# Attention scores as three rounded products, whole key blocks added on GpSimd, and a rewritten plan in a float32 chain of four attention layers

## The reference

```python
x = x + _L0_attn_a_ref(_layernorm(x, axis=-1), ...)   # "squared"
x = x + _L0_ffn_ref(_layernorm(x, axis=-1), ...)      # "gated"
x = x + _L0_attn_b_ref(_layernorm(x, axis=-1), ...)   # "mqa"
x = x + _L0_ffn_ref(_layernorm(x, axis=-1), ...)      # "gated"

# squared
q = _feature_map(q, gamma, beta)
k = _feature_map(k, gamma, beta)
q = q * D ** (-0.5)
attn = jnp.einsum('bqhd,bkhd->bhqk', q, k) ** 2
attn = jnp.where(mask, attn, 0.0)
o = jnp.einsum('bhqk,bkhd->bqhd', attn, v)
z = jnp.sum(attn, axis=-1)
o = o / (jnp.swapaxes(z, 1, 2)[..., None] + EPS)
return o.reshape(b, t, H * D) @ Wo.T

# gated
idx = jnp.argmax(gating, axis=-1)
k_shared = jnp.einsum('bth,bthd->btd', indicator, k)
v_shared = jnp.einsum('bth,bthd->btd', gating_top1, v)
att = jnp.einsum('bhqd,bkd->bhqk', q, k_shared) * (1.0 / math.sqrt(hd))
att = jax.nn.softmax(jnp.where(causal[None, None, :, :], att, -jnp.inf), axis=-1)
y = jnp.einsum('bhqk,bkd->bhqd', att, v_shared)

# mqa
scores = jnp.einsum('bqhd,bkd->bhqk', q, k) * scale
attn = jax.nn.softmax(jnp.where(causal[None, None], scores, min_val), axis=-1)
ctx = jnp.einsum('bhqk,bkd->bqhd', attn, v)
out = jnp.einsum('bsd,ed->bse', ctx, out_w) + out_b
```

## Time and profile before

| | us |
|---|---|
| median of 3 runs | 4801.09 |
| profiled execution | 4810.55 |
| its span | 4808.8 |
| PE busy / DVE busy / ACT busy / POOL busy | 4292.6 / 1770.6 / 1546.9 / 847.3 |
| mean granted PE clock, share of full speed | 0.961 |

### The profile page before, as it was taken

How to read it: one execution, slowest core, us unless ns; L and a number is a source line. 1 busy time by engine, 2 the same in 40 slices (tenths; PEclk the granted TensorE clock), 3 DMA queues, 4 the chain that set the end, 5 groups by cost and what they waited for, 6 DMA issues and landing times.

```text
span 4808.8 us, 76616 instructions
## 1 busy us (share of the span) xinstructions
PE 4292.6 (89%) x32674; PEld 1781.0 (37%) x32674; DVE 1770.6 (37%) x2666; ACT 1546.9 (32%) x1985; POOL 847.3 (18%) x1495
## 2 busy tenths in 40 slices
PE   6899999996999898898898989989899897988987
PEld 4343434333333333333333333333333333333333
DVE  1222212122544444434444443443443444444342
ACT  1433333340223323323333333332222233232333
POOL 1311212121101211202112221211112012011012
PEclk8999999998999999999999999999999999999999
DMA  1001010003000100101001010000001001010010
GB/s 62 18 1 36 18 36 18 18 18 102 18 1 1 54 1 23 32 1 38 16 23 32 12 43 1 25 30 26 28 1 46 9 1 54 1 37 17 1 36 27
DMA packets 63405, 115.67 MB, mean 24 GB/s; under 512 B 8672, under 2 KB 9184, under 8 KB 63072
## 3 DMA queue, kind: packets, MB, share of 16 engines
q1 hardware_dynamic: 63072, 110.77, 7.2%
HBM read 77.19 MB, written 33.55 MB: 23 GB/s over the span
## 4 chain that ended last, share of the span: by engine, by line
PE 58%; DVE 6%; issue 5%; ACT 3%; DMA 2%; POOL 2%; POOLq 0%; SPq 0%; DVEq 0%; ACTq 0%
PE banks L1085 14%; PE banks L1043 10%; PE banks L995 9%; PE banks L1027 8%; PE banks L988 7%; DVE maxima_soft L811 5%; PE banks L1024 3%; ACT probs_soft L732 3%; PE banks L1052 2%; PE banks L1184 2%; DMA tiles_soft<-out 1%; PE banks L1159 1%; PE banks L1094 1%; POOL tiles_soft L637 0%; POOL rest_soft L705 0%
## 5 line engine op out<-in xcount | busy, mean ns | idle before, releaser
L811 DVE TENSOR_REDUCE maxima_soft<-banks 128x2 f32<-128x1024 f32 (+3 forms) x1152 | 1036.6, 953 | 1309.8 <-PE banks L1052 828.6
L732 ACT ACTIVATE probs_soft<-banks 128x1024 f32<-128x1024 f32 (+1 forms) x960 | 848.5, 936 | 1252.4 <-PE banks L1027 1250.2
L1043 PE MATMUL banks<-k_soft,q_soft 32*128 32x512 f32 (+3 forms) x4608 | 547.0, 544 | 69.6 <-ACT probs_soft L732 67.6
L646 POOL TENSOR_SCALAR_AFFINE_SELECT probs_soft<-probs_soft 128x512 f32<-128x512 f32 x384 | 239.2, 635 | 1963.5 <-ACT probs_soft L732 1961.8
L1027 PE MATMUL banks<-q_soft,k_soft 32*128 32x512 f32 (+3 forms) x4608 | 487.1, 505 | 0.0
L1085 PE MATMUL banks<-probs_soft,v_soft 128*32 128x512 f32 (+3 forms) x4608 | 435.6, 497 | 13.4 <-ACT shift_soft L718 9.5
L1085 PE MATMUL banks<-probs_soft,ones 128*32 128x512 f32 (+3 forms) x4608 | 433.5, 495 | 0.0
L732 ACT ACTIVATE probs_squared<-banks 128x1024 f32<-128x1024 f32 (+1 forms) x320 | 282.8, 936 | 387.7 <-PE banks L1027 387.6
L1043 PEld LDWEIGHTS banks<-k_soft,q_soft 32*128 32x128 f32 x4608 | 187.1, 186 | 320.1 <-issue 302.3
L1024 PE MATMUL banks<-shift_soft,ones 32*128 32x512 bf16 (+3 forms) x2304 | 202.3, 339 | 113.9 <-DVE maxima_soft L811 100.9
L995 PE MATMUL banks<-g_wv,xnT_soft 128*128 128x512 f32 x512 | 251.4, 625 | 27.4 <-DVE inverse_soft L917 21.2
(11 more groups left out here) (151 smaller groups left out, 4218.7 us busy)
## 6 DMA issues: line engine op xcount, KB each, us to landing
tiles_soft<-out SPq DMA_DIRECT2D x96, 256.0 KB, 2.9
rest_soft<-out SPq DMA_DIRECT2D x96, 256.0 KB, 3.0
out<-rest_soft SPq DMA_DIRECT2D x96, 256.0 KB, 2.0
tiles_squared<-in_x SPq DMA_DIRECT2D x32, 256.0 KB, 2.9
rest_squared<-in_x SPq DMA_DIRECT2D x32, 256.0 KB, 2.9
out<-rest_squared SPq DMA_DIRECT2D x32, 256.0 KB, 2.0
raw_wq<-in_squared_wq SPq DMA_DIRECT2D x1, 1024.0 KB, 6.2
raw_wk<-in_squared_wk SPq DMA_DIRECT2D x1, 1024.0 KB, 8.5
```

The source lines that it names most:

```text
L646: ins = pool.affine_select(out=cells, in_=cells, compare_op=ALU.is_ge, fill=0.0, base=0, pattern=[[0, HG], [1, P]], channel_multiplier=-1)
L732: act.activation(slot(ph, n)[:, 2 * a:2 * a + 2, 0:width], score_pair(e, a)[:, :, 0:width], ACT.Exp if soft else ACT.Square, scale=SCALE). ...
L811: ins = dve.reduce_max(m["maxima"][:, ph % 2, 2 * a:2 * a + 2, t, p], score_pair(e, a)[:, :, col:col + P * blocks], AX_X)
L1043: ins = pe.matmul(psum[:, score_bank(e, i), col:col + P * blocks], m["q"][D * i:D * i + D, ph % NG, P * t:P * t + P], k_of(ph)[D * i:D * i ...
```

## The change

1. Queries and keys are kept as two float32r numbers, a rounded high part and the rest. ACT writes the high part from PSUM; DVE then subtracts it from the same bank and writes the low part, and only then is the bank free. Squares of them on POOL are an add and a multiply.
2. Each score product is three float32r products, high by high, high by low and low by high, in place of one float32 product. They stay in four 32-row groups.
3. No product is narrower than 256 columns: the narrow key products are widened to 256 and their surplus is not read. There are ten row bursts in place of nine, cut the same way.
4. For part B in the softmax layers POOL adds the four whole blocks of weights into `full_sum` (three adds of 128 by 2048), and "sm" for B is one block in place of four.
5. `SLOTS` 6 to 5, `TILES` 4 to 3, `Y_RING` 6 to 5, queries kept for three phases in place of four; the plan (`VALUES_AT`, `WEIGHT`, `spread`'s lists, `norm_events`) is rewritten, and "sm" B of a softmax phase is one whole unit.

```diff
-SLOTS = 6
-TILES = 4
-Y_RING = 6
+SLOTS = 5
+TILES = 3
+Y_RING = 5
 V_RING = 3
+QK_RING = 3
+PAIRS = [(HIGH, HIGH), (HIGH, LOW), (LOW, HIGH)]
...
-    (0, "A", [(1, 128, 384, 0), (3, 384, 128, 384)]),
-    (0, "A", [(2, 256, 256, 0)]),
+    (0, "A", [(1, 128, 384, 0)]),
+    (0, "A", [(2, 256, 256, 0), (3, 256, 256, 256)]),
...
-VALUES_AT = {"C": 1, "A": 8, "B": 14}
+VALUES_AT = {"C": 0, "A": 6, "B": 14}
...
-WEIGHT = {"keys": 1.3, "rows": 1.2, "av": 3.2, "sm": 3.2, "q": 3.5, ...
+WEIGHT = {"keys": 1.0, "rows": 0.9, "av": 3.2, "sm": 3.2, "q": 3.5, ...
...
+    elif soft and n > FULL[0]:
+        pool.wait_ge(sg.probs_ready, 2 * (of_kind[e] + 1))
+        if n == FULL[1] and ph:
+            wait_work(pool, ("sm", ph - 1, part))
+        elif n > FULL[1]:
+            pool.wait_ge(sg.probs_added, additions(ph, n) - 1)
+        before = slot(ph, FULL[0])[:] if n == FULL[1] else m["full_sum"][:]
+        pool.tensor_tensor(m["full_sum"][:], before, slot(ph, n)[:], ALU.add).then_inc(sg.probs_added, 1)
...
+    elif u in ("q", "q2", "k2", "ks", "kt"):
+        out, bias = split_target(e)
+        wait_work(act, e)
+        act.activation(out[:, HIGH], work[:, bank(e), :], ACT.Copy).then_inc(sg.high_ready, 1)
...
+    elif u in ("q", "q2", "k2", "ks", "kt"):
+        out, bias = split_target(e)
+        dve.wait_ge(sg.high_ready, high_parts[e])
+        ins = dve.tensor_tensor(out[:, LOW], work[:, bank(e), :], out[:, HIGH].bitcast(F32), ALU.subtract)
+        ins.then_inc(sg.work_free[bank(e)], 1)
...
-    for i in range(HG):
-        ins = pe.matmul(psum[:, score_bank(e, i), col:col + width],
-                        k_of(ph)[D * i:D * i + D, P * kb:P * kb + P],
-                        m["q"][D * i:D * i + D, ph % NG, CHUNK * c + q0:CHUNK * c + q0 + width],
-                        start=not soft, stop=True)
+    for x, (a, b) in enumerate(PAIRS):
+        for i in range(HG):
+            ins = pe.matmul(psum[:, score_bank(e, i), col:col + width],
+                            k_of(ph)[D * i:D * i + D, a, P * kb:P * kb + P],
+                            q_of(ph)[D * i:D * i + D, b, CHUNK * c + q0:CHUNK * c + q0 + width],
+                            start=(x == 0 and not soft), stop=(x == len(PAIRS) - 1))
...
+    if u == "sm" and soft and part == "B":
+        pe.wait_ge(sg.probs_added, additions(ph, FULL[-1]))
+        for i in range(HG):
+            ins = pe.matmul(out[D * i:D * i + D, :], k["ones"][:], m["full_sum"][:, i, :], start=True, stop=True)
+        products = []
```

More of the change, by code:

```diff
@@ L6 @@
 F32 = mybir.dt.float32
+F32R = mybir.dt.float32r
 BF16 = mybir.dt.bfloat16
@@ L73, with behind, blocks_seen @@
          "mxt", "rs", "rw", "out")
+def behind(c, kb, q0):
+    return max(P * (kb - TPC * c) - q0, 0)
 def parts_of(part):
     bursts = [n for n, burst in enumerate(KEY_BURSTS) if burst[1] == part]
-    products = sorted((kb, q0, width, n, col) for n in bursts for kb, q0, width, col in KEY_BURSTS[n][2])
-    return bursts, products
+    products = []
+    for n in bursts:
+        c = KEY_BURSTS[n][0]
+        for kb, q0, width, col in KEY_BURSTS[n][2]:
+            cut = behind(c, kb, q0)
+            products.append((kb, q0 + cut, width - cut, n, col + cut))
+    return bursts, sorted(products)
+def blocks_seen(t, p, blocks):
+    return min(blocks, t - TPC * p + 1)
 def norm_events(s):
-    events = [("stats", s, t) for t in range(3)]
+    events = [("load", s, t) for t in range(TILES)] + [("stats", s, t) for t in range(TILES - 1)]
     for t in range(NT):
-        if t + 3 < NT:
-            events.append(("stats", s, t + 3))
+        if t + TILES - 1 < NT:
+            events.append(("stats", s, t + TILES - 1))
         events.append(("ln", s, t))
@@ L588, in _ @@
         def _(sp):
-            stores = [Count() for _ in range(TILES)]
             for e in events:
```

241 lines of the change are left out of this document (141 added, 100 removed).

## The result

The changed kernel takes 4859.05 us (median of 4 runs, 4856.71 to 4860.78), the kernel before, run beside it, 4801.55 (4797.94 to 4805.5). The ratio is 1.0119, with a 95% interval of 1.0102 to 1.0137. Forecast were 4680 us and a range from 4550 to 4880: the time lies in the range, the direction was wrong, and faster had been given 0.72.

What follows compares the result with a forecast made beforehand. PE's own work was taken to set the time (busy 4292.6 us). Work -291, bank waits +62, split +25, adds +10, tiles +45, first act +25 make -124 us from 4810.55, so 4687, stated as 4680; range 4550 to 4880.

Steps and rivals of the forecast that it cites:

- +49 wider products: PE's key and row products: widening 128 columns to 256 adds work, netted inside the savings of -96 and -84 us.
- +45 tiles: Tile loads and outputs: three tiles need three rounds for eight, eleven stage changes at 4 us; bounds 0 and 100.
- +25 split: Projections of q and k: 184 DVE subtractions free the PSUM bank 0.8 us later; bounds 0 and 156 us.
- +25 first act: First act, ahead of `kvar`: a key chunk's square gains subtraction and add, 16 phases; bounds 0 and 64 us.
- +66 banks: PE's waits for score banks, from the rise in places short of other work; the prediction's whole term was +62 us.
- +10 adds: POOL's sums: each add mostly covered by PE's other work before sm B; bounds 0 and 240 us.
- I take the lower one: Rounded product at 512 columns: three passes at bf16's 0.23 us, 0.69 us, rather than 1.44 from today's instruction cost.
- The correction for the loads: Rounded products of 384 and 256 columns: held at 0.54 us by twelve weight loads, over their streaming 0.51 and 0.36.
- The named sign: Sign of being right: a rounded 512-column product of four heads takes 0.69 us from start to start.
- Counting those for banks from the order: PE work between bursts, set against DVE's or ACT's need: maxima 190 us short in 229 places, before 104 in 136.
- DVE's pace: Slower rival: DVE reaches row bursts one subtraction late, shortfall 394 us in place of 190, time 4880; chance 0.17.
- The rival with POOL and tiles: Rival: POOL and the tiles cost their upper halves, +150 us, giving 4810, no change or a little slower; chance 0.12.

Runs made afterwards that it cites:

- e3: The changed kernel with float32 scores without the split, and part B's sums on PE with six slots; plan, wide bursts and three tiles stay: 4914.97 us, ratio 1.0235.
- e2: The changed kernel with the sums of part B back on PE, four blocks, and six slots; rounded products stay: 4847.35 us, ratio 1.0079.
- e13: The changed kernel with two rounded products per score, low by high left out: 4674.70 us, ratio 0.9746.
- e4: The changed kernel with 320 bf16 matmuls without use, placed where PE was idle: 4840.96 us, ratio 1.0077.
- e9: e7 with the 320 bf16 matmuls without use added: 4743.00 us, ratio 0.9887.
- e7: e5 with av and sm later in the phase (VALUES_AT C 1, A 9, B 15): 4760.68 us, ratio 0.9919.
- e6: e3 with the key and row bursts of the kernel before, so without the widening: 4812.45 us, ratio 1.0030.
- e5: e2 with the key and row bursts of the kernel before, so without the widening: 4811.90 us, ratio 1.0029.
- e8: e7 with plain float32 scores in place of the rounded products: 4790.04 us, ratio 0.9978.
- e12: The changed kernel without POOL's adds; sm of part B reads the last block alone, three of four blocks left out: 4794.83 us, ratio 0.9988.

## Why the prediction was wrong

The forecast's sum can be cut by the three parts, since the profiled runs before, e3, e2 and after follow one another by one part each. In each part the change of the span is split in three. The traces record when the clock stood at which level; of PE's busy time in the low stretches (276.8 us before, 279.7 in e3, 388.6 in e2, 454.2 after) half is booked as the cost of the clock. What is left of the busy time is PE's work at full clock, and the rest of the span is idle. In us:

| part | forecast, work | measured, work at full clock | forecast, clock | measured, clock | forecast, waits | measured, idle | forecast, sum | measured, span |
|---|---|---|---|---|---|---|---|---|
| plan (before to e3) | +49 wider products | +69 | none | +1 | -2 banks, +45 tiles | +19 | +92 | +90 |
| rounded products (e3 to e2) | -222 | -178 | none | +54 | +25 split, +25 first act | +72 | -172 | -51 |
| sums on POOL (e2 to after) | -118 | -126 | none | +33 | +66 banks, +10 adds | +104 | -42 | +11 |
| all | -291 | -235 | none | +89 | +169 | +196 | -122 | +49 |

So of the 171 us between forecast and measurement some 89 are the clock, which had no term, 56 are work of PE that did not go (44 of them the price of the rounded products), and 27 are waits. The split can be trusted to a few us: from after to e13 it gives 248 us of work gone at full clock, and the passes left out are 246. That the plan comes out at +90 for +92 is partly luck: its products cost 20 us more than booked and its waits 24 less, and by the medians it costs 112.

**The price of a rounded product.** "I take the lower one": 0.69 us from bf16's 0.23 for each pass. The pass was right, as e13 shows. By the Trainium skill ("FP8 and Floating Point Precision", TensorE Precision Notes) true float32 is four passes through the array. The trace agrees: beyond 0.15 us a row product of 512 columns takes 4 x 0.23. That a rounded product is one pass the page does not say; e13 shows it. What was off is the fixed part, 0.06 to 0.1 us more for each product. The correction for the loads was wrong too: I held a product of 384 or 256 columns at the 0.54 us of its loads, and both grow by a whole pass between two products and three, so loads don't bind there. With the readings of the changed kernel (pairs 1.03 for 1.19, 0.80 for 0.82, 0.47 to 0.58, so 0.53 in the mean, for 0.66; rows 0.90 for 1.07, 0.73 for 0.86, 0.56 for 0.65) a phase saves 1.52 us for keys and 1.64 for rows against float32 products of the same widths, 176 us in all (178 by the clock record), not 222. The named sign, 0.69 us from start to start at 512 columns, came as 1.03 - 0.23 = 0.80 for a key product.

**The clock.** The forecast named a lower granted clock among what would prove it wrong, and had no term for it. It is the step that failed most: a term put at nothing without a reason, and it measured 89 us. Of PE's busy time 454 us lay in low stretches after the change and 277 before, and there were 96 such stretches for 60. The passes give back 54 us of their 178 this way and the blocks of sm 33 of their 126. From the other side, 320 matmuls without use put where PE stands idle lowered low by 138 us in e4 and by 96 in e9, and each run was 18 us faster, net of the added work. That shows that a part of it comes from idle stretches. Whether rounded products also bring the clock down by themselves is open: at nearly the same idle (516, 536, 528 us) low was 375 before, 372 in e3 and 485 in e7. In e3 and e7 the clock fell as often, 67 and 68 times, but a low stretch lasted 5.6 us in the mean in e3 and 7.2 in e7; no run changes the one and keeps the other.

**The waits of a faster PE.** When the products are shorter, what other engines do is not, so waits grow. e6 to e5 shows it purest: busy -85, idle +87, no gain. e8 to e7, where the order leaves more room: busy -80, idle +56, a gain of 29.

**The waits.** Their sum, 167 us forecast and 196 measured, was nearly right, though not in each part. Counting those for banks from the order held: 190 us forecast for the maxima and 167.1 measured; by the same count 144 for e2 and e3 (116.9 and 120.0 measured) and 33 for e7 (40.0). DVE's pace, the rival on the slow side, would have shown 394 us. The slow side came another way: PE's work fell, and the clock and the waits gave back more than that. The rival with POOL and tiles (0.12 for no change or a little slower) comes nearest, but neither cost its upper half, and its 4810 is a slip, since 4680 + 150 is 4830. That 4859 lies in the stated range is luck. The forecast had nothing for ACT's copies of the maxima (`shift_soft`, 44.5 us in all its rows, 9.5 before).

**The wider bursts.** Their price was netted in the terms for keys and rows. By the earlier trace rows it is 49 us of work, and by the count of the order 30 of waits; the runs give 102 by the medians (e6 to e3; 85 by the profiled spans), nearly all that the plan costs. I never asked what the change would do without them.

**Sums on POOL.** "I take +10", bounds 0 and 240: e12 measured 64. I priced the wait at the product with `full_sum`, and that is 3.8 us in all. That outputs and tiles stand behind the adds I said, without a price. An add took 4.53 us, not 5.1.

**Tiles and first act.** The +45 for three tiles did not come with the plan: PE waited 117.4 and 28.2 us for tiles of the softmax layers and of the first act before, 89.9 and 40.7 in e3, and 130.7 and 38.8 after, +24 in all, of which 12 go without the adds (e12). The first act's +25 nearly did: `key_square` went from 11.3 to 31.3 us. The split's +25 did: all of PE's waits for the low parts of q and k are 41.5 us, where its waits for ACT's copies of them were 17.0 before.

## What to carry to other kernels

Where the busiest engine already stands idle for a tenth of the span in short gaps, ask of each saving which gaps it widens and what clock follows: here a quarter of it was lost at best (e13) and all of it at worst (e6 to e5). Work that is moved to an idle engine costs what stands behind it in that engine's queue, not what waits for its result: read the queue one buffer further, since the wait is booked on the engine between. And try a change of several parts with each part undone: here the fastest version that computes all of the reference keeps the rounded products and most of the plan, and drops the widening and the sums.

## What the runs showed of the hardware

- A float32r matmul of 32 rows costs one pass, 0.23 us for four heads at 512 columns, and a row product of three 0.20 us beyond its passes at 512, 384 and 256 columns. At 128 columns a row product took 0.49 us in e5_narrow, less than the 0.56 at 256 but more than three passes and the fixed part would make (with a pass at 0.05, an estimate from the earlier trace rows, 0.35); float32 took 0.44.
- Twelve weight loads of 32 rows by 128 columns took 0.54 us, while one of them took 183 ns (median), so loads of different row groups overlap. By "TensorE: Matmul & The Clock Gate", LDWEIGHTS, of the Trainium skill a load takes its columns over 1.2 GHz, so 107 ns for 128 columns and 1.28 us for twelve in turn (an estimate by that rule); the trace decides for the overlap.
- POOL adds 128 by 2048 float32 in 4.53 us, while 128 by 512 take 1.27.
- PE work without use made the kernel faster twice, by 18 us each (e4 against after, e9 against e7), as the time at 1.2 GHz fell.
